# Cross attention values in turn over four groups of output rows, and expert numbers unpacked by explicit register operations

## What is computed

```python
x = x + _L0_attn_ref(_layernorm(x), Wq, bq, Wk, bk, Wv, bv, Wo, bo)   # 16 heads, 4 key groups, window 64
x = x + _L0_xattn_ref(_layernorm(x), ctx_2048, ctx_2048)              # 16 heads of 16, causal
x = x + _L0_ffn_ref(_layernorm(x), gate_w, sgate_w, w13, w2, shared_gate_up_w, shared_down_w)
```

```python
coef = jnp.sum(jnp.where(topk_ids == e, topk_w, 0.0), axis=-1)
h = _silu_and_mul(x @ w13_e.T)
acc = acc + (h @ w2_e.T) * coef[:, None]
```

## Time and profile before

| | us |
|---|---|
| median of 3 timed runs | 416.64 (412.84 to 417.04) |
| the profiled execution | 414.46 |
| its span, first to last instruction | 412.6 |
| TensorE busy | 364.2 (88%) |
| DVE busy | 254.8 (62%) |
| ACT busy | 180.3 (44%) |
| GpSimd busy | 157.5 (38%) |

### The profile page before, as it was taken

How to read it: one execution, slowest core, us unless ns; L and a number is a source line. 1 busy time by engine, 2 the same in 40 slices (tenths; PEclk the granted TensorE clock), 3 DMA queues, 4 the chain that set the end, 5 groups by cost and what they waited for, 6 DMA issues and landing times.

```text
span 412.6 us, 7763 instructions
## 1 busy us (share of the span) xinstructions
PE 364.2 (88%) x2198; PEld 260.7 (63%) x2198; DVE 254.8 (62%) x744; ACT 180.3 (44%) x538; POOL 157.5 (38%) x203
## 2 busy tenths in 40 slices
PE   7687998989899895986997949999999999999883
PEld 3345675757586864755866725666666666668662
DVE  2647799797979689876254633444444444443894
ACT  1052867676758476674424312333333333332220
POOL 2923416262625324566537500333333333333000
PEclk9898999999989999999798978999999999999997
DMA  7990000878676671111102143667666666662901
GB/s 237 350 387 2 2 1 2 249 221 255 202 251 207 213 247 39 41 67 52 54 26 94 66 143 93 195 191 206 192 202 201 186 208 198 193 195 98 390 24 51
DMA packets 43029, 64.25 MB, mean 156 GB/s; under 512 B 5251, under 2 KB 31892, under 8 KB 42484
## 3 DMA queue, kind: packets, MB, share of 16 engines
q1 hardware_dynamic: 38356, 52.45, 41.0%
q0 software_dynamic: 3792, 10.49, 6.7%
q10 hardware_dynamic: 848, 0.92, 0.9%
HBM read 34.88 MB, written 28.97 MB: 155 GB/s over the span
## 4 chain that ended last, share of the span: by engine, by line
PE 38%; issue 24%; DVE 16%; POOL 13%; ACT 4%; DMA 3%; SPq 1%; POOLq 0%; DVEq 0%
POOL y_picks L595 11%; PE bank L1414 10%; PE bank L1328 5%; PE bank L1343 5%; ACT probs L637 3%; PE bank L1319 3%; DVE neg_max L874 3%; PE bank L1283 3%; PE bank L1314 2%; DVE x L1243 2%; PE bank L1370 2%; PE bank L1302 2%; DVE q_stk L846 1%; PE bank L1397 1%; PE bank L1384 1%
## 5 line engine op out<-in xcount | busy, mean ns | idle before, releaser
L595 POOL DMA_INDIRECT y_picks<-yb,ids x47 | 45.1, 959 | 93.7 <-DVE yb L1215 93.1
L637 ACT ACTIVATE probs<-bank,neg_max 128x128 f32<-128x128 f32 x256 | 69.9, 414 | 16.0 <-DVE neg_max L874 16.0
L1669 PE MATMUL bank<-w,xbt 128*128 x188 | 69.2, 492 | 1.0 <-ACT xbt L764 0.8
L1208 DVE TENSOR_TENSOR hb<-sg,bank 128x176 f32<-128x176 f32 x47 | 15.9, 338 | 67.8 <-issue 23.8
L772 ACT ACTIVATE sg<-bank 128x176 f32<-128x176 f32 x47 | 14.9, 317 | 84.7 <-PE bank L1669 84.7
L1669 PEld LDWEIGHTS bank<-w,xbt 128*128 128x128 f32 x188 | 32.7, 193 | 26.9 <-issue 17.3
L1689 PE MATMUL bank<-w,hbt 128*128 128x256 f32 x188 | 48.2, 380 | 0.0
L874 DVE TENSOR_REDUCE neg_max<-bank 128x4 f32<-128x512 f32 x64 | 41.0, 683 | 11.3 <-PE bank L1319 11.3
L539 POOL DMA_INDIRECT x_slots<-x,slots x32 | 32.8, 1025 | 23.1 <-DVE slots L1003 14.2
L1328 PE MATMUL bank<-ident,probs 128*128 128x128 f32 x256 | 36.6, 282 | 2.1 <-ACT probs L637 2.1
L880 DVE COPY probs_t<-bank 128x512 f32<-128x512 f32 x47 | 31.9, 685 | 7.5 <-PE bank L1328 7.3
(11 more groups left out here) (176 smaller groups left out, 717.0 us busy)
## 6 DMA issues: line engine op xcount, KB each, us to landing
x_slots<-zero_b SPq DMA_DIRECT2D x16, 1056.0 KB, 10.6
w<-w_in_dram SPq DMA_DIRECT2D x47, 256.0 KB
xb<-x_slots SPq DMA_DIRECT2D x47, 132.0 KB, 2.4
w<-w_in_dram SPq DMA_DIRECT2D x4, 1408.0 KB, 10.8
yg<-y_picks SPq DMA_DIRECT2D x8, 512.0 KB, 7.0
sw_raw<-shared_in_dram SPq DMA_DIRECT2D x6, 384.0 KB, 3.5
ctx_sb<-ctx_in_dram SPq DMA_DIRECT2D x1, 1024.0 KB, 12.0
out_dram<-x SPq DMA_DIRECT2D x8, 128.0 KB, 1.8
```

The source lines that it names most:

```text
L595: pool.indirect_dma_start(y_picks[:, :], bass.IndirectOffsetOnAxis(ids[:, n:n + 1], 0), yb[:, n % RB, :], None).then_inc(yb_placed[n % RB] ...
L637: ins = act.activation(probs[:, g, j, :], ps_s[g][:, 128 * j:128 * j + 128], ACT.Exp, bias=neg_max[:, g, j:j + 1])
L1669: ins = pe.matmul(ps_gu[n % 2][:, 0:GU], xbt[:, n % 2, k, :], w13[:, bass.ds(e, 1), k, :].rearrange("p e n -> p (e n)"), start=k == 0, sto ...
```

## The change

**In the cross values**, `values` is now for self attention alone, and a new `cross_values(c)` issues the 16 matmuls with the head j outside and the group g inside. It first waits for both counters of `probs_t` copies, where the two halves each waited for their own. It adds 2 to `values_psum[CROSS]` at the last matmul, where each half added 1. It is called where the two halves were called. **In `unpack`**, shift and mask are written as two register operations on a register of their own, for every block.

```diff
             def values(kind, b, u):
 
                 pe.wait_ge(probs_t_ready[kind][u], 2 * b + 2)
-                pe.wait_ge(v_ready if kind == SELF else c_pad_ready, b + 1)
+                pe.wait_ge(v_ready, b + 1)
                 for g in (2 * u, 2 * u + 1):
                     out_rows = slice(PAD * g, PAD * g + PAD)
-                    if kind == SELF:
-
-                        ins = pe.matmul(ps_o[out_rows, :], v_pad[:, g, :],
-                                        probs_t[:, g, :, :].rearrange("p j n -> p (j n)"), start=True, stop=True)
-                        continue
-                    for j in range(BLK):
+                    ins = pe.matmul(ps_o[out_rows, :], v_pad[:, g, :],
+                                    probs_t[:, g, :, :].rearrange("p j n -> p (j n)"), start=True, stop=True)
+                ins.then_inc(values_psum[kind], 1)
+
+            def cross_values(c):
+
+                for u in range(2):
+                    pe.wait_ge(probs_t_ready[CROSS][u], 2 * c + 2)
+                pe.wait_ge(c_pad_ready, c + 1)
+                for j in range(BLK):
+                    for g in range(TILES):
+                        out_rows = slice(PAD * g, PAD * g + PAD)
                         ins = pe.matmul(ps_o[out_rows, 128 * j:128 * j + 128], c_pad[:, j, g, :], probs_t[:, g, j, :],
                                         start=True, stop=True)
-                ins.then_inc(values_psum[kind], 1)
+                ins.then_inc(values_psum[CROSS], 2)
...
-                    values(CROSS, c, 0)
-                    values(CROSS, c, 1)
+                    cross_values(c)
...
             def unpack(n):
 
-                experts[n] = pe.snap((packed[n // PACK] >> (4 * (n % PACK))) & (NE - 1), min_val=0, max_val=NE - 1)
+                r = pe.alloc_register(f"expert{n}")
+                pe.reg_alu(r, packed[n // PACK], 4 * (n % PACK), ALU.logical_shift_right)
+                pe.reg_alu(r, r, NE - 1, ALU.bitwise_and)
+                experts[n] = pe.snap(r, min_val=0, max_val=NE - 1)
```

More of the change, by code:

```diff
@@ L1616, in _ @@
             pe.wait_ge(attn_ready[CROSS], B - 1)
-            values(CROSS, B - 1, 0)
-            values(CROSS, B - 1, 1)
+            cross_values(B - 1)
             rows_of(1)
```

## The result

| | before | after |
|---|---|---|
| median of 4 timed runs, us | 416.84 (412.84 to 417.33) | 398.88 (397.73 to 400.30) |
| the profiled execution, us | 414.46 | 397.73 |
| its span, us | 412.6 | 395.9 |

The ratio is 0.9591 with a 95% interval of 0.952 to 0.9661: about 18 us less. The two profiled executions differ by 16.7 us.

The account below looks back on a forecast made before the run. Cross values stand on the attention chain, and register operations idle weight loads in expert blocks. Gains of 7.7 and 8.5 us sum to 16.2, giving 398.3 or 400.4 by starting time; forecast 399.5 us, 8-in-10 range 395 to 406.

Parts of the forecast that it names:

- The length of a set: Cross values, 32 loads and 32 matmuls: from 2.39 to 1.05 us with groups in turn, a gain of 1.34 us.
- Set 1: Cross values at 55.42 us: DVE's norm is already later than the scores, so gain 0.
- Sets 2 to 4: Cross values before DVE's row maxima, which waited 1.35 us for scores: 3 x 1.34 = 4.02 us gained.
- Sets 5 and 6: Cross values at 139.51 and 166.00 us, with DVE waits of 3.12 and 1.64 us behind: 2.68 us gained.
- Set 7: Cross values at 184.88 us: GpSimd's context copy waits for them, but GpSimd is busy until 186.95; gain 0.45 us.
- Set 8: Cross values at 205.34 us: the merged wait for the last probability copy costs 0.79 us, leaving 0.55 us gained.
- The registers: Expert blocks: 84 shift and mask operations leave the idle time before weight loads; 8.5 us gained, period about 2.49 us.
- Only A: Rival: only the cross values' new order works, registers still cost time before the load; 408.9 us, chance 0.05.
- only B: Rival: only register unpacking works, cross values stay at 2.39 us a set; 408.1 us, chance 0.05.
- SyncE does not bound the blocks: Rival claimed SyncE or a transfer holds blocks at 2.60 us, losing 4.8 us: 404.3 us, chance 0.08.
- Loads of different groups of output rows: Rival: these weight loads don't overlap matmuls, cross values take 3.64 us a set; 418 us, chance 0.02.
- The clock: TensorE in attention: one to three low-clock stretches more or fewer, about 1 us each; rival with all low, 442, chance 0.02.

Follow-up runs that it names:

- the experiment with pairs: Changed kernel, but cross values take groups in turn only within pairs (0 and 1, then 2 and 3), each pair behind its own wait: 404.68 us, ratio 0.9774.
- the experiment with the late scatters: Changed kernel, but at the sixth cross attention GpSimd makes the deviation and keeps the rows before the four scatters: 396.94 us, ratio 0.9529.
- the experiment with explicit registers at the use: Changed kernel, but the same two register operations are issued inside block_up behind its waits, in every block: 407.36 us, ratio 0.9787.

## Why the prediction was right, step by step

The forecast was 399.5 us; the median is 398.88. The gain was forecast as 16.2 us, and it is 16.7 between the two profiles, 18.0 between the medians and 16.0 at equal time at the lower level. That the time itself came within 0.6 us is partly luck, since the forecast was set between two starting times 2.2 us apart and the runs of one kernel spread over 5 us.

- **The length of a set** was taken as 1.05 us between bounds of 1.00 and 2.39; it is 1.01. The self values were the right model. Nothing of the step of 0.11 us that might have come from the queue shows; by the reading of the experiment with pairs, four groups in turn never fill a group's queue.
- **What survives of it.** Set 1: 0 forecast, 0 measured. Sets 2 to 4: 1.34 each forecast, 1.38 measured, with DVE's wait gone. Sets 5 and 6: 1.34, measured 1.35 and 1.33. Set 7: 0.45 against 0.51, with GpSimd's scatters as what limits it, which the experiment with the late scatters shows. Set 8: 0.55 against 0.30. This term was mis-sized: it counted the end of the last copy, but not what lies between it and the first matmul, 0.28 us, of which 0.11 is a satisfied wait that stands behind the last one. Sum: 7.7 forecast, 7.63 measured, the too small gain of a set offsetting set 8.
- **The registers.** 8.5 us from 84 operations, 8.25 measured; period 2.496 against 2.501, in 44 blocks the 0.25 us that are missing. The count was slightly off: between the loads that bound these 44 blocks stand 81 of the 86 operations, so one cost 0.102 us; those of the first three blocks lie ahead. The idle time ahead of the load, forecast at 0.13 us, is 0.15. The experiment with explicit registers at the use shows that the move does it.
- **The rivals.** "Only A" and "only B" were forecast at 408.9 and 408.1 from the median of 416.64, as kernels of their own too: 407.33 and 406.36 measured, from 415.2. SyncE does not bound the blocks: it still waits 11.6 us in 30 of them, 0.26 us each without the longest, where 0.24 was forecast. Loads of different groups of output rows do overlap matmuls: 12 loads and 8 matmuls in the first 0.20 us of a set. The sentence of the Trainium skill ("TensorE: Matmul & The Clock Gate", section "The mechanism") that ties this overlap to different row groups does not hold for these sets, which share all 128 rows.
- **The clock.** One to three stretches more or fewer were allowed; between the profiles it is one fewer at set 4, one longer at set 8 and another place at the end, 0.5 us in sum. Not forecast was how long a stretch can get: 10.2 us in the changed kernel.

## What to carry to other kernels

Matmuls with few output columns of the array (32 here) should be issued with the column groups in turn, one matmul for each group: with eight records a group, a group that got them all first held the next one off until half of them had started. Register arithmetic for an address belongs ahead of the wait, not between the wait and the load: it cost 0.1 us an operation there and nothing a block earlier. And of waits that stand in a row on one engine, the one satisfied last should be the last, which was worth about 0.11 us for the one that stood behind it here.

## What the runs showed of the hardware that was not expected

- Each group of 32 output rows took four records ahead, as the starts read: the next groups' records came in when a group had four of its eight left to finish (second pair at 0.47 us, the first pair's fifth at 0.46), and sets of 32 records took 2.39, 1.47 and 1.01 us with one, two and four groups in turn.
- Satisfied waits are not free behind an unsatisfied one: 0.26 to 0.28 us from the last copy's end to the first matmul with one behind it, 0.15 us with none.
- The time at the lower clock explains most of the spread between executions of one kernel: 0.26 us of time for each us of it, from 22 to 43 us in the kernel before, and half a us for each where TensorE is busy throughout (6.43 us at a mean clock of 0.73, 8.22 at 0.57 for the same work).
